# A row inverse Fourier transform on TensorE cut into 64x64 tiles by even and odd frequency

## What is computed

```python
xn = _ln(xp, ln1w, ln1b)                       # over the 64 channels
xf = jnp.fft.rfft2(xn, axes=(1, 2), norm='ortho')
...                                            # two complex 64x64 mixes with relu, a threshold mask
xs = jnp.fft.irfft2(xc, s=(H, W), axes=(1, 2), norm='ortho')
x = residual + jnp.transpose(xs, (0, 3, 1, 2))
xp2 = _ln(jnp.transpose(x, (0, 2, 3, 1)), ln2w, ln2b)
h = jax.nn.gelu(xp2 @ mw1 + mb1, approximate=False)
m = h @ mw2 + mb2
return x + jnp.transpose(m, (0, 3, 1, 2))
```

## Time and profile before

| | |
|---|---|
| median of 3 runs | 3488.26 us (3488.07 to 3488.36) |
| the profiled execution | 3488.49 us |
| its span, first to last instruction | 3486.2 us |
| mean granted TensorE clock | 0.962 of full speed |
| busy: PE, DVE, ACT, POOL | 93%, 68%, 63%, 48% |

### The profile page before, as it was taken

One profiled execution on the slowest core, in us unless ns is written; L12 is line 12 of the kernel. 1 busy time (PEld: TensorE's weight loads), 2 busy tenths in 40 slices (PEclk: granted clock), 3 DMA queues, 4 the chain that ended last, 5 costly groups with the idle time before them and its releaser, 6 DMA issues. The chain is left out here.

```text
span 3486.2 us, 52802 instructions
## 1 busy us (share of the span) xinstructions
PE 3236.5 (93%) x18285; PEld 1963.5 (56%) x18285; DVE 2363.6 (68%) x4046; ACT 2197.1 (63%) x3477; POOL 1689.7 (48%) x1421
## 2 busy tenths in 40 slices
PE   6945699999999999999999999999999999979689
PEld 2735465657565656464646565757565656344257
DVE  4956667777777676766666767676767675536667
ACT  3955566666666666767676666575757575646468
POOL 4435546464646455555464655545454643310242
PEclk7967899999999999999999999999999999989789
DMA  9860001010202111313120111111111111457898
GB/s 328 274 200 19 37 31 66 32 67 31 67 31 67 37 66 39 120 43 142 50 88 37 65 41 61 43 55 43 55 43 55 43 55 43 169 178 204 273 292 241
DMA packets 250280, 334.10 MB, mean 96 GB/s; under 512 B 22304, under 2 KB 195616, under 8 KB 242608
## 3 DMA queue, kind: packets, MB, share of 16 engines
q1 hardware_dynamic: 241664, 315.29, 26.8%
q0 software_dynamic: 7904, 15.57, 1.6%
q10 hardware_dynamic: 464, 0.02, 0.0%
HBM read 188.06 MB, written 142.74 MB: 95 GB/s over the span
## 5 line engine op out<-in xcount | busy, mean ns | idle before, releaser
L1576 ACT ACTIVATE images<-a_wide,a_up_b 128x1024 f32<-128x1024 f32 x512 | 569.8, 1113 | 253.0 <-PE a_wide L1766 249.7
L1766 PE MATMUL a_wide<-images 64*128 64x512 f32 x2048 | 579.0, 641 | 26.6 <-ACT images L1576 25.9
L1318 POOL TENSOR_TENSOR images<-a_o,a_mag 128x256 f32<-128x256 f32 (+1 forms) x512 | 360.4, 730 | 371.6 <-DVE a_mag L1426 368.8
L1276 POOL TENSOR_TENSOR images<-images,a_stat 128x512 f32<-128x512 f32 x256 | 267.2, 1044 | 544.6 <-DVEq L1473 528.1
L1777 PE MATMUL a_result<-images 128*64 128x512 f32 x2048 | 495.9, 605 | 1.8 <-DVE images L1437 1.8
L1406 DVE TENSOR_TENSOR a_o<-a_bank,a_mix_b 128x512 f32<-128x512 f32 (+1 forms) x272 | 180.9, 665 | 248.7 <-PE a_bank L1723 241.8
L1739 PEld LDWEIGHTS a_bank<-a_dft_h,a_g 128*128 128x128 f32 x2080 | 272.4, 191 | 129.0 <-issue 129.0
L1766 PEld LDWEIGHTS a_wide<-images 64*128 64x128 f32 x2048 | 156.6, 185 | 289.2 <-issue 259.4
L1437 DVE TENSOR_TENSOR images<-a_result,images 128x512 f32<-128x512 f32 x256 | 175.7, 686 | 205.6 <-PE a_result L1792 205.2
L1777 PEld LDWEIGHTS a_result<-images 128*64 128x64 f32 x2048 | 124.4, 136 | 322.4 <-issue 318.8
L1459 DVE TENSOR_REDUCE a_stat<-a_sq 128x16 f32<-128x1024 f32 x240 | 290.7, 1211 | 22.1 <-ACT a_sq L1610 20.4
(11 more groups left out here) (206 smaller groups left out, 6109.9 us busy)
## 6 DMA issues: line engine op xcount, KB each, us to landing
rows<-images SPq DMA_DIRECT2D x112, 512.0 KB, 2.6
images<-rows SPq DMA_DIRECT2D x105, 512.0 KB, 3.7
box_xc<-in_x SPq DMA_DIRECT2D x16, 1024.0 KB, 16.5
box_x<-in_x SPq DMA_DIRECT2D x64, 256.0 KB, 4.5
turned<-box_o SPq DMA_DIRECT2D x64, 256.0 KB, 3.6
images<-turned SPq DMA_DIRECT2D x16, 1024.0 KB, 13.0
planes<-box_work SPq DMA_DIRECT2D x64, 256.0 KB, 3.5
box_xc<-planes SPq DMA_DIRECT2D x16, 1024.0 KB, 18.8
```

The source lines that it names most:

```text
L1276: G.tensor_tensor(rows(y2[:, i % 2]), x[:, row:row + HB], r[:, :, None].broadcast_to([P, HB, C]), ALU.mult).then_inc(s_y2, 1)
L1318: ins = G.tensor_tensor(y[n % 2][:, :, to].rearrange("p c k -> p k c"), o2[:, j % 3, lo:4, r], mask[:, lo:4], ALU.mult)
L1576: A(hidden[:, i % 2, j], wide[:], ACT.Gelu, bias=up_b2[:, l, j:j + 1]).then_inc(s_hid, 1)
L1766: mm = M(wide[:, half * BANK:(half + 1) * BANK], up_fold[cs, l, j * P:(j + 1) * P], yc[cs, i % 2], start=True, stop=True)
```

## The change

`backward` is split by the parity of the row frequency. The rows of `dft_h`, `dft_hi` and of the mirror matrix are reordered so that even `kh` stand in partitions 0 to 63 and odd `kh` in 64 to 127. A cosine of row `64 - h` is that of row `h`, with the other sign where `kh` is odd (a sine: where `kh` is even). So the sums over even and over odd `kh`, for 64 columns of `dft_hi`, give all 128 rows when they are added and subtracted. A part now has eight channels, and each channel four matmuls with 64 rows of contraction, 64 stationary columns and 64 moving columns. Even and odd results go to two banks. ScalarE copies the even bank to SBUF (`xf` or `o1`, both free at that time) and one row to `iy`; VectorE adds and subtracts the odd bank, in five operations, into `iy`. Eight parts, two in a slot, use the four banks as two pairs: a part waits for VectorE and ScalarE to be done with the part two before it.

```diff
@@ constants()
+    kh = row_frequencies()                       # even ones first, then odd ones
+    out[DFT_H] = out[DFT_H][:, kh]
+    quarter = HALF // 2
+    out[DFT_HI][:, 0:quarter] = np.cos(turn[kh, 0:quarter])
+    out[DFT_HI][:, quarter:HALF - 1] = np.sin(turn[kh, P - quarter + 1:])
+    out[DFT_HI][:, HALF - 1] = np.where(kh % 2, np.sin(turn[kh, P - quarter]), np.cos(turn[kh, quarter]))
...
+    mirror = mirror[kh][:, kh]
@@ slots
-U_INVERSE, U_FORWARD, U_SPECTRUM, U_BACKWARD, U_NEXT, U_END = 0, 4, 20, 39, 55, 59
+U_INVERSE, U_FORWARD, U_SPECTRUM, U_BACKWARD, U_NEXT, U_END = 0, 4, 20, 39, 47, 51
-        return U_BACKWARD + 4 * (slot - BACKWARD_SLOT)
+        return U_BACKWARD + 2 * (slot - BACKWARD_SLOT)
@@ buffers
-        iy = g[:].rearrange("p k r c -> p (k r c)")[:, 0:C * P].rearrange("p (h c) -> p h c", c=C)
+        iy = g[:].rearrange("p k r c -> p (k r) c")
+        def even_rows_of(i):
+            return (o1 if i % 2 else xf)[:].rearrange("p (c h) -> p h c", h=HALF)
+        def of_kh(i, odd_kh):
+            return bank[2 * (i % 2) + odd_kh].rearrange("p (c h) -> p h c", h=HALF)
@@ VectorE
                 def backward(n, i):
-                    if i % 2 == 0:
-                        dve.wait_ge(s_ih, GROUPS * n + i + 1)
-                        V.tensor_copy(iy[:, :, 4 * i:4 * i + 4], four(bank[i % 4]).rearrange("p c h -> p h c")
-                                      ).then_inc(s_iy[0], 1)
+                    e, o, cs, quarter = even_rows_of(i), of_kh(i, 1), slice(8 * i, 8 * i + 8), HALF // 2
+                    dve.wait_ge(s_ih, C // 8 * n + i + 1)
+                    dve.wait_ge(s_even_rows, C // 8 * n + i + 1)
+                    for t in range(2):
+                        lo = (0, P - quarter + 1)[t]
+                        V.tensor_tensor(iy[:, lo:lo + quarter - t, cs], e[:, quarter * t:quarter * (t + 1) - t],
+                                        o[:, quarter * t:quarter * (t + 1) - t], ALU.add)
+                    V.tensor_copy(iy[:, P - quarter, cs], o[:, HALF - 1])
+                    V.tensor_tensor(iy[:, quarter + 1:HALF + 1, cs][:, ::-1], e[:, 0:quarter], o[:, 0:quarter], ALU.subtract)
+                    V.tensor_tensor(iy[:, HALF + 1:P - quarter, cs][:, ::-1], o[:, quarter:HALF - 1], e[:, quarter:HALF - 1],
+                                    ALU.subtract).then_inc(s_iy[0], 1)
@@ ScalarE
                 def backward(n, i):
-                    if i % 2 == 1:
-                        act.wait_ge(s_ih, GROUPS * n + i + 1)
-                        A(iy[:, :, 4 * i:4 * i + 4], four(bank[i % 4]).rearrange("p c h -> p h c"), ACT.Copy
-                          ).then_inc(s_iy[1], 1)
+                    cs, quarter = slice(8 * i, 8 * i + 8), HALF // 2
+                    act.wait_ge(s_ih, C // 8 * n + i + 1)
+                    if i >= 2:
+                        act.wait_ge(s_iy[0], C // 8 * n + i - 1)
+                    A(even_rows_of(i)[:], of_kh(i, 0), ACT.Copy).then_inc(s_even_rows, 1)
+                    A(iy[:, quarter, cs], of_kh(i, 0)[:, HALF - 1], ACT.Copy).then_inc(s_iy[1], 1)
@@ TensorE, backward(n, i)
-                    if i >= 4:
-                        pe.wait_ge(s_iy[i % 2], GROUPS // 2 * n + i // 2 - 1)
-                    for c in range(4):
-                        mm = M(bank[i % 4][:, c * P:(c + 1) * P], y[n % 2][:, 4 * i + c, :], dft_hi[:], start=True, stop=True)
+                    if i >= 2:
+                        pe.wait_ge(s_iy[0], C // 8 * n + i - 1)
+                        pe.wait_ge(s_iy[1], C // 8 * n + i - 1)
+                    for c in range(8):
+                        for part in range(2):
+                            to = slice(part * HALF, (part + 1) * HALF)
+                            for odd_kh in range(2):
+                                kh = slice(odd_kh * HALF, (odd_kh + 1) * HALF)
+                                mm = M(bank[2 * (i % 2) + odd_kh][to, c * HALF:(c + 1) * HALF], y[n % 2][kh, 8 * i + c, to],
+                                       dft_hi[kh, 0:HALF], start=True, stop=True)
                     mm.then_inc(s_ih, 1)
```

More of the change, by code:

```diff
@@ L59, in z_rows, with row_frequencies @@
     return np.arange(P).reshape(2, UNITS // B, U_CHUNKS, -1).transpose(1, 2, 0, 3).reshape(-1)
+def row_frequencies():
+    return np.arange(P).reshape(HALF, 2).T.reshape(-1)
 def constants():
@@ L72, in constants @@
     out[DFT_H][HALF + 1:] = -np.sin(turn[HALF + 1:])
-    out[DFT_HI] = np.cos(turn)
-    out[DFT_HI][:, HALF + 1:] = np.sin(turn[:, HALF + 1:])
+    kh = row_frequencies()
[4 more added lines that the diff above has]
+    out[DFT_HI][:, HALF - 1] = np.where(kh % 2, np.sin(turn[kh, P - quarter]), np.cos(turn[kh, quarter]))
     out[DFT_W][:, :KW] = np.cos(turn[:, :KW]) / P
@@ L1088, in afno_layers @@
         s_top, s_masked, s_sym, s_ends = (sem(n) for n in ("top", "masked", "sym", "ends"))
-        s_ih, s_iy = sem("ih"), [sem("iy_dve"), sem("iy_act")]
+        s_ih, s_even_rows, s_iy = sem("ih"), sem("even_rows"), [sem("iy_dve"), sem("iy_act")]
         s_iw, s_odd, s_even, s_x, s_x_up = (sem(n) for n in ("iw", "odd", "even", "x", "x_up"))
@@ L1679, in inverse @@
                     if j == 0:
-                        pe.wait_ge(s_iy[0], GROUPS // 2 * (n + 1))
-                        pe.wait_ge(s_iy[1], GROUPS // 2 * (n + 1))
+                        pe.wait_ge(s_iy[0], C // 8 * (n + 1))
+                        pe.wait_ge(s_iy[1], C // 8 * (n + 1))
                     elif j >= 2:
```

## The result

The changed kernel takes 3579.49 us (3579.15 to 3579.89, 4 runs) where the kernel before, on the same chip, takes 3488.31 (3488.07 to 3489.90): a ratio of 1.026 (95% interval 1.0243 to 1.0278), 91 us slower. The forecast was 3485 in a range of 3473 to 3513.

What follows compares the result with a forecast made beforehand. TensorE's passes were taken to bound each `backward` stage. Twelve ordinary stages gain 12.0 us, the first loses 2, so 10 off 3488 gives 3478; 7 for clock falls gives 3485, range 3473 to 3513.

Steps and rivals of the forecast that it cites:

- PE's work: TensorE in a `backward` stage: 512 passes of 64 columns, four at once, 0.93 us a part, 7.4 us a stage.
- rival of two tiles: TensorE's tiles: only two run at once, 1.86 us a part, giving 3531 us; chance 0.08.
- floor of 25 ns from pass to pass: TensorE's issue: pass starts never closer than about 25 ns, 1.60 us a part, giving 3513 us.
- The ring: Loop of waits in `backward` between PE, ScalarE's copy and VectorE: 3.44 us for two parts, bounding the stage instead of PE.
- VectorE's price: VectorE's five operations a part: 1.51 us first start to last end, VectorE taken for 1.43 us a part.
- The bound from line 1411: Upper bound for VectorE's operations a part, from a copy of 128 scattered elements taking 0.372 us: 2.11 us.
- ScalarE's 0.60: ScalarE's copy of the even bank in each part: 0.60 us.
- the dear case: `backward` stage with VectorE as bound: 18.6 us to `inverse` at 1.78 us a part, 21.3 at 2.11.
- The clock: PE's clock falling to half behind gaps: six stretches in 15 stages at 1.2 us, 7 us; forecast case, chance 0.33.
- The dear VectorE: Rival: VectorE's operations cost more for strides and reversed rows, giving 3497 us, or 3530 at 2.11 a part; chance 0.16.
- the rival of slow passes: TensorE's instruction supply: 512 short passes a stage given out too slowly, giving 3505 to 3525 us; chance 0.12.
- The tail: VectorE's last operations in a stage, hidden under 3.99 us of MLP work before `inverse`; uncovered they would cost 2.3 us.

Runs made afterwards that it cites:

- e2: The changed kernel with the even bank's SBUF buffer and the PSUM banks laid row by row, eight channels side by side: 3501.27 us.
- e1: The changed kernel with ScalarE copying the even bank in the order in which it lies, VectorE's reads unchanged: 3559.56 us.
- e6: The changed kernel with one more 512-column matmul, its result unused, behind each of parts 1 to 6: 3553.68 us.
- e5: The changed kernel with only the SBUF buffer of the even bank laid row by row, PSUM as before: 3501.53 us.
- e7: e2 with a filler matmul, result unused, behind parts 1, 3 and 5: 3493.36 us, ratio 1.0009.
- e3: The changed kernel with each small 64x64 matmul run twice, same result: 3736.06 us.
- e8: e2 with two pieces of MLP work moved from behind the eight parts to between them: 3493.52 us.
- e4: The changed kernel with eight full-array matmuls a part (128 weight columns, 64 moving) in place of the tiles, row transform not computed: 3703.15 us.

## Why the prediction was wrong

**PE's work: right.** 512 passes a stage, 0.93 to 1.05 us a part at full clock, the copy 1.22 us after the first tile, hand-overs of 0.05. The rival of two tiles fell, and so did a floor of 25 ns from pass to pass: it is 15 ns here.

**The ring as the new bound: right.** PE's idle time ahead of its tiles is put down to VectorE's last subtraction: 104.4 us in 87 times, 6.5 us a stage in five or six gaps, where the prediction said six gaps of some 6 us. That this sum came out is in part luck: parts at the half clock took 2 us and not 1, and filled what longer waits had opened. The stage's length is that of the ring and of VectorE.

**VectorE's price: the step that failed.** It is the sentence "I take 1.43, because the copy of now also writes scattered runs (of four elements, the new ones have eight) at no price". The copy of before writes scattered runs, but it steps through no SBUF operand with 256 bytes from element to element. The bound from line 1411, 2.11 us a part, was the right one: 2.07 was measured from start to start (1250.69 to 1252.76). That copy writes single elements 512 bytes apart in SBUF, which makes it the row of before that was like the new operations. Once the buffer lies row by row, the five operations take 1.47 us from first start to last end (e2), where the kernel after has 2.16 and the forecast 1.51. ScalarE's 0.60 was mis-sized for the same reason: 1.07, worth 20 us (e1). With the prediction's formula for the dear case, 1.88 + 8 x 2.11 + 2 x 1.18 + 0.13 = 21.3 us, and 0.47 more for the copy, 21.7; e6, where the clock is out of it, has 22.06.

The Trainium skill, SBUF — State Buffer (Door 1: The DMA port swizzle, the note on SBUF "cachelines"), has lines of 16 bytes in SBUF and a penalty for each access that moves to another one. The runs agree for the buffer: an addition of 256 elements takes 0.42 us where it reads runs of eight neighbours, and 0.60 at a step of 256 bytes. The same note has 8-byte lines in PSUM and slow matmuls for what isn't contiguous there. The runs don't agree: in e2 the matmuls write with a step of 8 elements, and 128 passes take 2.10 us for 2.09; VectorE's reads from PSUM cost the same in e2 and e5.

**The clock: wrong in number and in kind.** Six falls of some 3.4 us were taken, as at 1638 us. It fell in all 16 stages and stayed down for 13.65 us in the stage shown, in which more gaps follow; with the gaps filled it stays up (e6). The term of 7 us was thus mis-sized: it costs at least some 25.8 us (e6), the upper bound of the prediction (15 x 1.7 = 25). "The clock falls in every stage" was named as what would make it wrong.

**Rivals that feed each other.** The dear VectorE was priced at 3530 with 5 us for the clock, and the clock's falls with a cheap VectorE. But the first gap is 2.54 us in the kernel after and 1.36 in e2, where the clock stays up in most ordinary stages: the dear operations bring the falls. Only both together give the time. To the 3530 came also the three stages with a fill, which lost 5.6 us each where nothing was assumed, and the first, which lost 6.1 and not 2.

**The sum.** From the kernel after to e6 25.8 us go and from e6 to e7 60.3. How much of the latter is ScalarE's, no run with the clock up shows; the 20 us of e1 were measured with the clock falling. The split depends on the order (e6 has three fillers more), its sum of 86.1 doesn't. There remain 3.4 us over the kernel before (3493.36 against 3489.99, ratio not told from 1), where the prediction had some 10 below. Of these 13 us, ordinary stages make up 9 (12 x (18.22 - 17.47)) and those with a fill 5; the first stage, 18.1 for 19.9, gives back 2.

**The missing gain: the rival of slow passes, in part.** It had one packet of instructions more for each 128 passes, rightly, and was held unlikely because a packet takes 1.15 us and the ring 3.4. The transfer time was the wrong measure: in e3 128 passes come each 3.6 us or later, no faster than the forecast ring of 3.44 uses them. In e2 and e7 14 to 15 us of PE's time go there, and e7's best stage has 17.25 while the mean is 18.2. It hardly showed in the kernel after (1.4 us), since VectorE was slower still.

**The tail: right.** In all stages but the first it lies under the MLP; where e8 took the cover away, `inverse` waited for VectorE.

## What to carry to other kernels

When work is moved from a full engine to others, price their operations by the layout of each operand, input and output, and not by size: a row that writes scattered runs says nothing of one that steps through a buffer. Lay the intermediate buffer out so that the innermost loop runs over neighbours; here one line of layout gave back some 78 us, the clock's share included (the kernel after against e5). And when a change turns a full TensorE into one that waits, count the lower clock and the many small instructions as costs that begin together with the gaps.

## What the runs showed of the hardware

- A step of 256 bytes in an SBUF operand: 0.60 us for 0.42 (VectorE, 256 fp32 read), 1.07 for 0.60 (ScalarE, 512 fp32 written). The same step in PSUM and reversed rows cost nothing.
- Four 64x64 tiles run at once, 15 ns from pass to pass, but PE gets some 256 instructions each 3.6 us and more (e3); this shows as idle time for "issue". The Trainium skill, Runtime: NRT & Kernel Launch (Instruction fetch mechanics), has blocks of 256 instructions too, and their fetch as hidden behind the rate of issue: the first agrees with the packets here, the second doesn't agree with 163.6 us of PE's idle time in e3.
- A matmul added as a filler made the kernel faster (e6, 25.8 us). A busy PE alone did not bring the clock back: 24.99 of 25.10 us at a mean of 0.59 (e4).
- A pass with weights of 128 columns and 64 moving ones took 0.113 us from start to start (e4), about as long as one with 128 moving columns (0.112).
